# A local-attention stage in blocks of 32 queries and 64 keys: half as many probability transposes, twice as many small value products

## The chip, the cores and the metric

The kernel runs on one core of a Trainium2 chip. The metric is the device time of one execution in microseconds, the median of three runs. A profiled execution gives a span (first to last instruction) and a trace. Engines: PE is TensorE (matrix products and transposes), PEld its weight loads, DVE VectorE, ACT ScalarE, POOL GpSimd, SP the engine that issues the DMAs here.

## The reference, cut to what matters

A first attention layer, then six layers of a larger attention and a feed-forward block. The change touches the first attention alone:

```python
# x: (2, 1024, 128), 16 heads of 8, window of 32 keys
qkv = x @ W_attn + b_attn
q, k, v = jnp.split(qkv, 3, axis=-1)
scores = jnp.einsum('bhtd,bhsd->bhts', q, k) * scale
mask = causal & (j >= i - 32)
scores = jnp.where(mask[None, None], scores, -jnp.inf)
attn = jax.nn.softmax(scores, axis=-1)
out = jnp.einsum('bhts,bhsd->bhtd', attn, v)
return out.transpose(0, 2, 1, 3).reshape(b, t, c) @ W_proj + b_proj
```

A query sees itself and the 32 keys before it, so a block of 32 queries sees 64 keys, and a block of 64 queries sees 96.

## The kernel before, in words

The 2048 rows are 16 tiles of 128 (`TILES`). The first attention works through them in a software pipeline: the order on each engine is written out by hand in that engine's `tile_first`, and semaphores (names with `a_`) join the engines. Tiles 0, 1, 14 and 15 are unrolled, the rest is a loop of two tiles (`tiles`). `t` is the tile, `p` its buffer (t mod 2), `G` one of two groups of eight heads, `b` one of two groups of four inside it.

For one tile, in order of data:

- PE `project_first` (L1089, L1090) makes q, k and v from the input that ACT copied (`copy_first`, L433). ACT `qkv_first` moves them out: q (L463), k (L467), v (L471). v goes to `v_nat`, with two buffers. POOL `split_keys` (L348) makes four masked copies of the keys.
- SP `move_first` copies v from `v_nat` to `vw1`, where each query half finds its 96 keys on partitions 0 to 95: two DMAs for the tile itself (L238, L239), and one (L242) with its last 32 rows, for the next tile. L242 waits until the tile before is fully weighed (`a_pv`), since its buffer is that tile's. ACT may write v of tile t+2 into `v_nat` only when L242 of tile t has landed (`a_before`).
- PE `scores_first` adds a mask through an identity product in bf16 (L1052, 384 columns, one for each of two PSUM banks), then the scores (L1059): 2 halves of 64 queries x 2 banks, each with 4 heads x 96 keys.
- DVE `maxima_first` (L721) takes the row maxima, ACT `exps_first` (L478) one exponential per head (128x96) with its sum, 16 a tile.
- PE `transpose_probs_first` (L1067) transposes each head's 128x96 probabilities, 16 a tile, in four groups; DVE `probs_first` (L729) copies each group of four out of PSUM.
- PE `weigh_first` (L1080) multiplies by the values: a product per head and half, 96 keys deep, 64 queries x 8 columns, 32 a tile. All results of a tile stand in one PSUM bank, `OB`.
- DVE `heads_out_first` (L735, L738) divides by the sums, PE transposes (L1095), ACT moves it out (`oT`, L487), PE projects (L1099), DVE adds the bias (L745).

A product of f32 operands appears in the trace as two records, a transpose as one.

On PE one step of the pipeline is: project(t+2), transpose probabilities of (t, G=0), weigh (t-1, G=1), scores (t+1, G=0), transpose out (t-1), scores (t+1, G=1), project out (t-1), weigh (t, G=0), transpose probabilities of (t, G=1). On ACT it is: exponentials of (t, 0) second half, (t, 1), then q, k, v of t+2, the copy of the input, `oT` of t-1, and exponentials of (t+1, 0) first half.

Of the kernel before, what the change touches and what calls it, by code (L numbers as in the profile page):

```python
# [6 lines left out]
TILES = B * N // P  # L7
# [8 lines left out]
SPAN = HALF + WIN  # L16

# [17 lines left out]
def build(nc, x, Wa, ba, Wp, bp, Wqkv, Wo, scales, W1, W2, par, rope, ident, identb, mask, select, out):  # L35
# [3 lines left out]
    with ctx:  # L39
# [26 lines left out]
        msk = sb("msk", [P, TILES, SPAN], mybir.dt.uint16)  # L66

# [46 lines left out]
        pT = sb("pT", [SPAN, 8, P])  # L114
# [20 lines left out]
        PROB1, PT1 = (prob[:, :, :], prob1), (pT[:, :, :], pT1)  # L135
# [19 lines left out]
        a_seen, a_before = [sem("a_seen0"), sem("a_seen1")], [sem("a_before0"), sem("a_before1")]  # L155
        a_linv, a_o, a_ot_full, a_ot_evac = sem("a_linv"), sem("a_o"), sem("a_ot_full"), sem("a_ot_evac")
# [9 lines left out]
        pt_full, pt_evac, pv_done = sem("pt_full"), sem("pt_evac"), sem("pv_done")  # L166
        v_seen = [sem("v_seen0"), sem("v_seen1")]
# [10 lines left out]
        CONSTS = 16 * 9  # L178
# [40 lines left out]

        block = ctx.enter_context(nc.Block())  # L220
# [3 lines left out]
        def _(eng):  # L224
# [4 lines left out]
            for dst, src in ((idf[:, :], ident), (idb[:, :], identb), (wa, Wa), (wp, Wp),  # L229
                             (bias_c[:, :], ba), (bias_p, bp), (msk[:, :, :], mask),  # L230
                             (rope0[:, :, :, :], rope), (sel[:, :], select)):
# [67 lines left out]
        def _(eng):  # L299
# [8 lines left out]
            nc.gpsimd.memset(vw1[0:WIN, 0, 0, :], 0.0).then_inc(init_done, 1)  # L308
# [106 lines left out]
        def _(eng):  # L415
# [43 lines left out]
            def qkv_first(t, p):  # L459
# [9 lines left out]
                at_least(eng, a_seen[p], seen(t, p) - 32)  # L469
                at_least(eng, a_before[1 - p], t * 8 - (0 if p == 0 else 8))  # L470
# [12 lines left out]
            def heads_out_first(t):  # L483
# [3 lines left out]
                nc.scalar.activation(oT[:, 0, 0:P], RING[4][:, 0:P], ACT.Identity, bias=bias_c[:, 2:3]).then_inc(a_ot_evac, 1)  # L487
# [58 lines left out]
            exps_first(0, 0, 0, 0)  # L546

            def tile_first(t, n, p, opening, closing):

                ahead = not (isinstance(n, int) and n >= TILES - 2)  # L550
                exps_first(t, p, 0, 1)
# [9 lines left out]
                if not closing:  # L561
                    exps_first(t + 1, 1 - p, 0, 0)
            tiles(eng, tile_first, lambda t, n, p: heads_out_first(t), 0)
# [126 lines left out]
        def _(eng):  # L690
# [27 lines left out]
            def maxima_first(t, p, G):  # L718
                for b in range(2):
                    eng.wait_ge(a_s, t * 2 + (G + 1))  # L720
                    nc.vector.tensor_reduce(nmax[:, p, 8 * G + 4 * b:8 * G + 4 * b + 4],  # L721
                                            S1[G][b][:, 0:4 * SPAN].rearrange("p (h k) -> p h k", h=4),
                                            AX.X, ALU.max, negate=True).then_inc(a_max, 1)

            def probs_first(t, G, b):

                eng.wait_ge(a_pt_full, t * 4 + (2 * G + b + 1))
                at_least(eng, a_pv, t * 2 + (G - 1))
                nc.vector.tensor_copy(PT1[G][:, 4 * b:4 * b + 4, :],  # L729
                                      RING[4 + 2 * b][0:SPAN, :].rearrange("p (h q) -> p h q", h=4)).then_inc(a_pt_evac, 1)  # L730
# [12 lines left out]
            def residual_first(t, n):  # L743
                eng.wait_ge(a_wo, t + 1)
                nc.vector.tensor_tensor(y_nat[:, n, :], RING[6][:, 0:C], bias_p, ALU.add).then_inc(a_y, 1)  # L745
# [88 lines left out]
            def tile_first(t, n, p, opening, closing):  # L834
                ahead = not (isinstance(n, int) and n >= TILES - 2)
                probs_first(t, 0, 0)
# [4 lines left out]
                probs_first(t, 0, 1)  # L841
                if not closing:
                    maxima_first(t + 1, 1 - p, 0)
                if not opening:
                    residual_first(t - 1, n - 1)
                if not closing:
                    maxima_first(t + 1, 1 - p, 1)
                if not opening:
                    eng.wait_ge(a_y, t)
                    nc.vector.bn_stats(stats[:, n - 1, :], y_nat[:, n - 1, :])  # L850
                probs_first(t, 1, 0)
                probs_first(t, 1, 1)
# [177 lines left out]
        def _(eng):  # L1030
# [15 lines left out]
            def scores_first(t, n, p, G):  # L1046
# [4 lines left out]
                for b in range(2):  # L1051
                    nc.tensor.matmul(S1[G][b][:, 0:4 * SPAN], idb[:, :].bitcast(bf16),  # L1052
                                     msk[:, n, :].bitcast(bf16).rearrange("p (o k) -> p o k", o=1).to_broadcast([P, 4, SPAN]),
                                     start=True, stop=False, skip_group_check=True)
# [9 lines left out]
            def transpose_probs_first(t, G, b):  # L1064
                eng.wait_ge(a_p, t * 4 + (2 * G + b + 1))
# [397 lines left out]
```

## Time and profile before

| | us |
|---|---|
| runs: median (lowest to highest) | 2088.4 (2085.85 to 2089.87) |
| profiled execution: its own time | 2085.3 |
| its span | 2083.4 |
| first attention: first projection to last residual | 19.6 to 161.6 |
| PE busy over the whole span | 1911.9 (92%) |
| ACT, DVE, POOL busy | 1597.1, 1582.3, 1670.8 |

The first attention is 142 us of 2083.4, under 7%. The granted clock of PE is a column of its own in several views: 1.00 is 2.4 GHz, 0.50 is 1.2 GHz. "Issue" is time in which an engine waited for nothing that the profile shows. Records of matrix products are pipelined: one that is 200 ns long does not hold the engine for 200 ns, so the distance from start to start of two groups is the measure used below.

### The profile page before, as it was taken

How to read it: one execution, taken by the hardware profiler on the slowest of the kernel's cores; microseconds unless marked ns; L12 is line 12 of the kernel's file. 1: busy time of each engine (PE TensorE's matmuls, PEld its weight loads, DVE VectorE, ACT ScalarE, POOL GpSimd, SP SyncE). 2: the span in 40 equal slices, each digit the busy share in tenths (PEclk: the TensorE clock that was granted, in tenths of full speed). 3: DMA queues.
4: the chain of work that ended last, by engine and by line, in shares of the span. 5: the costliest groups of instructions: out<-in, count | busy, mean ns of one | idle time of the engine just before them, and what ended most of it. 6: DMA issues, size and time to landing. Idle time of an engine off the chain costs nothing.

```text
span 2083.4 us, 67375 instructions
## 1 busy us (share of the span) xinstructions
PE 1911.9 (92%) x22192; PEld 1446.7 (69%) x22192; DVE 1582.3 (76%) x4021; ACT 1597.1 (77%) x5607; POOL 1670.8 (80%) x1264
## 2 busy tenths in 40 slices
PE   6994999988999988999988999998999999999987
PEld 4662777874777774777774777774777774777773
DVE  5766888867888866788866788876788876888875
ACT  5872888875888874888884888884888884888873
POOL 3224999967999966999966999976899975999971
PEclk8995999999999999999999999999999999999999
DMA  3001212212112112111211211111211110211110
GB/s 118 12 12 27 69 46 49 56 32 68 49 45 58 48 32 71 48 45 45 58 34 49 69 46 45 45 47 40 75 49 45 45 47 20 65 46 45 45 44 21
DMA packets 44548, 99.44 MB, mean 48 GB/s; under 512 B 7344, under 2 KB 24208, under 8 KB 43504
## 3 DMA queue, kind: packets, MB, share of 16 engines
q1 hardware_dynamic: 44400, 97.59, 18.0%
q8 instruction: 78, 1.28, 0.2%
q14 instruction: 70, 0.57, 0.1%
HBM read 19.59 MB, written 1.05 MB: 10 GB/s over the span
## 4 chain that ended last, share of the span: by engine, by line
PE 71%; issue 11%; POOL 8%; ACT 5%; DVE 4%; DMA 0%; ACTq 0%; POOLq 0%; DVEq 0%
PE bank L1162 9%; PE bank L1175 8%; PE bank L1189 7%; PE bank L1210 7%; PE bank L1155 7%; PE bank L1191 6%; PE bank L1190 6%; PE bank L1196 6%; PE bank L1146 3%; ACT kT L533 2%; PE bank L1291 2%; POOL rn L327 2%; POOL ropeL L360 2%; POOL tsum L329 2%; PE bank L1202 2%
## 5 line engine op out<-in xcount | busy, mean ns | idle before, releaser
L327 POOL TENSOR_TENSOR rn<-n2c,half_neg 128x8 f32<-128x8 f32 x384 | 636.7, 1658 | 80.3 <-DVE n2c L807 79.6
L495 ACT ACTIVATE prob<-bank,nmax 128x96 f32<-128x96 f32 x1536 | 502.6, 352 | 131.8 <-DVE nmax L757 131.6
L329 POOL TENSOR_TENSOR tsum<-tc_,ts_ 128x512 f32<-128x512 f32 x384 | 489.6, 1275 | 0.0
L332 POOL TENSOR_TENSOR w_nat<-tsum,rn 128x512 f32<-128x512 f32 x384 | 401.3, 1045 | 37.7 <-POOL tsum L329 15.1
L800 DVE TENSOR_REDUCE n<-nat 128x8 f32<-128x512 f32 x384 | 262.3, 683 | 140.4 <-ACT nat L511 128.1
L495 ACT ACTIVATION_READ_ACCUMULATOR prob<-bank,nmax 128x1 f32 x1536 | 333.2, 217 | 0.0
L757 DVE TENSOR_REDUCE nmax<-bank 128x4 f32<-128x384 f32 x384 | 196.3, 553 | 155.4 <-PE bank L1155 147.4
L504 ACT ACTIVATE pT<-bank 96x512 f32<-96x512 f32 x384 | 230.6, 601 | 74.5 <-PE bank L1162 72.2
L1189 PE MATMUL bank<-w_hi,xs 128*128 128x512 f32 x576 | 275.7, 479 | 12.4 <-DVE ts_ L810 9.8
L1162 PE MATMUL bank<-idf,prob 128*96 128x128 f32 x1536 | 246.0, 284 | 44.1 <-ACT kT L533 28.3
L810 DVE TENSOR_TENSOR ts_<-bank,ropeL 128x256 f32<-128x256 f32 x768 | 286.1, 414 | 0.0
L803 DVE TENSOR_TENSOR tc_<-bank,ropeL 128x512 f32<-128x512 f32 x384 | 261.3, 680 | 0.0
L511 ACT ACTIVATE nat<-bank 128x512 f32<-128x512 f32 x384 | 232.9, 607 | 33.6 <-PE bank L1191 30.0
L1196 PE MATMUL bank<-idf,w_nat 128*128 128x128 f32 x1536 | 237.9, 278 | 13.1 <-POOL w_nat L332 11.6
L1196 PEld LDWEIGHTS bank<-idf,w_nat 128*128 128x128 f32 x1536 | 181.4, 141 | 90.7 <-issue 32.8
L1162 PEld LDWEIGHTS bank<-idf,prob 128*96 128x96 f32 x1536 | 159.5, 128 | 106.6 <-ACT kT L533 79.2
L1190 PE MATMUL bank<-w_lo,xs 128*128 128x512 f32 x576 | 229.2, 398 | 0.0
L1191 PE MATMUL bank<-w_hi,xs_lo 128*128 128x512 f32 x576 | 229.2, 398 | 0.0
L1175 PE MATMUL bank<-vspace,pT 96*64 96x64 f32 x6144 | 221.2, 225 | 0.0
L1175 PEld LDWEIGHTS bank<-vspace,pT 96*64 96x64 f32 x6144 | 194.7, 138 | 31.4 <-issue 20.7
L1210 PE MATMUL bank<-oT,wo 128*128 128x128 f32 x1536 | 207.3, 279 | 4.1 <-ACT oT L524 4.1
L1210 PEld LDWEIGHTS bank<-oT,wo 128*128 128x128 f32 x1536 | 189.5, 194 | 6.0 <-ACT oT L524 5.5
(124 smaller groups left out, 3349.2 us busy)
## 6 DMA issues: line engine op xcount, KB each, us to landing
vspace<-v_nat SPq DMA_DIRECT2D x96, 384.0 KB, 4.0
vspace<-v_nat SPq DMA_DIRECT2D x96, 256.0 KB, 3.4
vspace<-v_nat SPq DMA_DIRECT2D x95, 128.0 KB, 2.2
nat<-w_qkv SPq DMA_DIRECT2D x5, 1536.0 KB, 8.4
wo<-w_o SPq DMA_DIRECT2D x6, 512.0 KB, 3.9
w<-w SPq DMA_DIRECT2D x6, 341.0 KB, 3.1
shared<-w_qkv SPq DMA_DIRECT2D x1, 1536.0 KB, 8.6
w<-w SPq DMA_DIRECT2D x6, 192.0 KB, 3.0
```

The lines of the kernel that those rows point to most:

```text
L327: nc.gpsimd.tensor_tensor(rn[:, r, :], n2c[:, r, :], half_neg[:, 0:8], ALU.pow).then_inc(pool_step, 1)
L329: nc.gpsimd.tensor_tensor(tsum[:, r, :], tc_[:, r, :], ts_[:, r, :], ALU.add).then_inc(pool_step, 1)
L332: nc.gpsimd.tensor_tensor(w_nat[:, r, :].rearrange("p (h d) -> p h d", d=D), tsum[:, r, :].rearrange("p (h d) -> p h d", d=D), rn[:, r, :] ...
L495: last = nc.scalar.activation(prob[:, 4 * b + i, :], SB[b][:, i * SPAN:(i + 1) * SPAN], ACT.Exp, bias=nmax[:, p, 8 * G + 4 * b + i:8 * G + ...
L810: last = nc.vector.tensor_tensor(ts_[:, r, :].rearrange(heads3, d=D)[:, :, lo:lo + D // 2], pj[:, :].rearrange(heads3, d=D)[:, :, hi:hi + ...
L1162: last = nc.tensor.transpose(RING[at][0:SPAN, i * P:(i + 1) * P], prob[:, 4 * b + i, :], idf[:, :])
L1175: last = nc.tensor.matmul(OB[qs, a:a + D], pT[:, 4 * b + i, qs], vw[:, p, half, head * D:(head + 1) * D], start=True, stop=True, skip_grou ...
L1189: nc.tensor.matmul(PJ[x % 2][:, :], xs[:, p, :], hi, start=True, stop=False)
L1190: nc.tensor.matmul(PJ[x % 2][:, :], xs[:, p, :], rest, start=False, stop=False)
L1191: nc.tensor.matmul(PJ[x % 2][:, :], xs_lo[:, p, :], hi, start=False, stop=True).then_inc(pj_ready, 1)
L1196: last = nc.tensor.transpose(RING[at][:, i * P:(i + 1) * P], w_nat[:, j % 2, i * P:(i + 1) * P], idf[:, :])
L1210: last = nc.tensor.matmul(YB[:, 0:P], wo[:, 4 * G + i, :], oT[:, G, i * P:(i + 1) * P], start=G == 0 and i == 0, stop=G == 1 and i == 3)
```

## The change

The first attention goes to blocks of 32 queries and 64 keys (`BLOCKS` = 4, `SEEN` = 64).

- Mask and scores have 4 x 64 = 256 columns instead of 384; the score products of a group are 8 instead of 4 (four blocks x two banks), 32 queries each. A second mask table `mskB` is loaded at the start, one more DMA.
- Exponentials and maxima work on 64 keys per head. ACT puts the probabilities of head i of b=0 and head i of b=1 side by side, so that one 128x128 transpose takes two heads: 8 transposes a tile instead of 16, 2 DVE copies instead of 4. Partitions 0 to 63 hold the heads of b=0, 64 to 127 those of b=1.
- Value products are one per head and block, 64 keys deep, 32 queries x 8 columns: 64 a tile instead of 32. The two partition halves write the same bank, so they go in two turns (b=0, then b=1), and the second waits for the end of the first (`a_pv_half`). A semaphore `pv_begun` is incremented ahead of each turn, and nobody waits for it.
- `move_first` fills the blocks of values with 8 DMAs instead of 2, and the rows for the next tile with 2 instead of 1.
- The order on PE, ACT and DVE is written anew: the transposes of (t, 0) wait for all eight exponentials of their group, and the two turns of (t-1, 1) stand on either side of scores (t+1, 0). On ACT both halves of the exponentials of (t+1, 0) now end the step. `oT` and the projected output change places in the PSUM banks 4 and 6.

```diff
-        vw1 = first_only(4 * C)[0:SPAN, :].rearrange("p (r h c) -> p r h c", r=2, h=2)
-        prob1 = first_only(8 * SPAN).rearrange("p (h k) -> p h k", h=8)
-        pT1 = first_only(8 * P)[0:SPAN, :].rearrange("p (h q) -> p h q", h=8)
+        vw1 = first_only(4 * C).rearrange("p (r w c) -> p r w c", r=2, w=BLOCKS)
+        prob1 = first_only(8 * SEEN)
+        pT1 = first_only(4 * P).rearrange("p (h q) -> p h q", h=4)
...
                 eng.wait_ge(a_v, t + 1)
                 at_least(eng, a_pv, t * 2 - 2)
-                eng.dma_start(vw1[WIN:SPAN, p, 0, :], v_nat[0:HALF, p, 0:C]).then_inc(a_seen[p], 16)
-                eng.dma_start(vw1[:, p, 1, :], v_nat[WIN:P, p, 0:C]).then_inc(a_seen[p], 16)
+                for b in range(2):
+                    cols = slice(b * C // 2, (b + 1) * C // 2)
+                    eng.dma_start(vw1[b * SEEN + WIN:(b + 1) * SEEN, p, 0, :], v_nat[0:WIN, p, cols]).then_inc(a_seen[p], 16)
+                    for w in range(1, BLOCKS):
+                        eng.dma_start(vw1[b * SEEN:(b + 1) * SEEN, p, w, :], v_nat[(w - 1) * WIN:(w + 1) * WIN, p, cols]
+                                      ).then_inc(a_seen[p], 16)
                 if not last:
                     at_least(eng, a_pv, t * 2)
-                    eng.dma_start(vw1[0:WIN, 1 - p, 0, :], v_nat[P - WIN:P, p, 0:C]).then_inc(a_before[1 - p], 16)
+                    for b in range(2):
+                        eng.dma_start(vw1[b * SEEN:b * SEEN + WIN, 1 - p, 0, :],
+                                      v_nat[P - WIN:P, p, b * C // 2:(b + 1) * C // 2]).then_inc(a_before[1 - p], 16)
...
-                at_least(eng, a_pt_full, t * 4 + (2 * G + b - 3))
+                at_least(eng, a_pt_full, t * 2 + (G - 1))
                 for i in range(4):
-                    head = 8 * G + 4 * b + i
+                    head, slot = 8 * G + 4 * b + i, 2 * i + b
                     last = nc.scalar.activation(
-                        PROB1[G][:, 4 * b + i, :], S1[G][b][:, i * SPAN:(i + 1) * SPAN], ACT.Exp,
+                        PROB1[G][:, slot * SEEN:(slot + 1) * SEEN], S1[G][b][:, i * SEEN:(i + 1) * SEEN], ACT.Exp,
...
-                for half in range(2):
-                    qs, ks = slice(half * HALF, (half + 1) * HALF), slice(half * HALF, half * HALF + SPAN)
+                for w in range(BLOCKS):
+                    qs, ks = slice(w * WIN, (w + 1) * WIN), slice(w * WIN, w * WIN + SEEN)
                     for b in range(2):
                         rows = slice((2 * G + b) * ROWS, (2 * G + b + 1) * ROWS)
-                        last = nc.tensor.matmul(S1[G][b][qs, 0:4 * SPAN].rearrange("p (h k) -> p h k", h=4),
+                        last = nc.tensor.matmul(S1[G][b][qs, 0:4 * SEEN].rearrange("p (h k) -> p h k", h=4),
...
-            def transpose_probs_first(t, G, b):
-                eng.wait_ge(a_p, t * 4 + (2 * G + b + 1))
+            def transpose_probs_first(t, G):
+
+                eng.wait_ge(a_p, t * 4 + (2 * G + 2))
                 for i in range(4):
-                    last = nc.tensor.transpose(RING[4 + 2 * b][0:SPAN, i * P:(i + 1) * P], PROB1[G][:, 4 * b + i, :], idf[:, :])
+                    last = nc.tensor.transpose(RING[4 + 2 * G][:, i * P:(i + 1) * P],
+                                               PROB1[G][:, 2 * i * SEEN:2 * (i + 1) * SEEN], idf[:, :])
...
+            def weigh_first(t, p, G, b):
+
+                if b == 0:
+                    at_least(eng, a_pv, t * 2 + G)
+                    eng.wait_ge(a_pt_evac, t * 2 + (G + 1))
+                    if G == 0:
+                        at_least(eng, a_o, t)
+                        eng.wait_ge(a_seen[p], seen_block(t, p))
+                        at_least(eng, a_before[p], prev_block(t, p))
+                else:
+                    eng.wait_ge(a_pv_half, t * 2 + (G + 1))
+
+                eng.sem_inc(pv_begun, 1)
+                rows = slice(b * SEEN, (b + 1) * SEEN)
+                for i in range(4):
+                    head = 8 * G + 4 * b + i
+                    for w in range(BLOCKS):
+                        qs = slice(w * WIN, (w + 1) * WIN)
+                        last = nc.tensor.matmul(OB[qs, head * DA:(head + 1) * DA], PT1[G][rows, i, qs],
+                                                vw1[rows, p, w, (4 * G + i) * DA:(4 * G + i + 1) * DA], start=True, stop=True,
...
```

On PE, the rest of the step of tile 1 after its projections, before. `vspace` and `prob` hold probabilities, `msk` the mask, `shared` the keys:

```order
L1067 MATMUL bank<-idf,prob 96x128 x8
L1080 MATMUL bank<-vspace 64x8 x16
L1052 MATMUL bank<-msk,idb 128x384 x2
L1059 MATMUL bank<-shared,qT 64x384 x4
L1095 MATMUL bank<-idf,o_nat 128x128
L1052 MATMUL bank<-msk,idb 128x384 x2
L1059 MATMUL bank<-shared,qT 64x384 x4
L1099 MATMUL bank<-vspace,oT 128x128
L1080 MATMUL bank<-vspace,pT 64x8 x16
L1067 MATMUL bank<-idf,vspace 96x128 x8
```

The same step of the changed program:

```order
L1085 MATMUL bank<-idf,prob 128x128 x4
L1107 MATMUL bank<-vspace 32x8 x16
L1069 MATMUL bank<-mskB,idb 128x256 x2
L1076 MATMUL bank<-shared,qT 32x256 x8
L1107 MATMUL bank<-vspace 32x8 x16
L1069 MATMUL bank<-mskB,idb 128x256 x2
L1076 MATMUL bank<-shared,qT 32x256 x8
L1122 MATMUL bank<-idf,o_nat 128x128
L1107 MATMUL bank<-vspace,pT 32x8 x16
L1126 MATMUL bank<-vspace,oT 128x128
L1107 MATMUL bank<-vspace,pT 32x8 x16
L1085 MATMUL bank<-idf,vspace 128x128 x4
```

Two groups of products became four turns, and both groups of scores stand ahead of the transpose of the output. On SP, the DMAs of values of tiles 0 and 1, before:

```order
L238 DMA vspace<-v_nat 64x128
L239 DMA vspace<-v_nat 96x128
L242 DMA vspace<-v_nat 32x128
L238 DMA vspace<-v_nat 64x128
L239 DMA vspace<-v_nat 96x128
L242 DMA vspace<-v_nat 32x128
```

The same two tiles of the changed program:

```order
L253 DMA vspace<-v_nat 32x64
L255 DMA vspace<-v_nat 64x64 x3
L253 DMA vspace<-v_nat 32x64
L255 DMA vspace<-v_nat 64x64 x3
L260 DMA vspace<-v_nat 32x64 x2
L253 DMA vspace<-v_nat 32x64
L255 DMA vspace<-v_nat 64x64 x3
L253 DMA vspace<-v_nat 32x64
L255 DMA vspace<-v_nat 64x64 x3
L260 DMA vspace<-v_nat 32x64 x2
```

Three DMAs a tile became ten, and the release of a `v_nat` buffer (L242, now L260) is two DMAs long.

## Rows read from the trace of the kernel before

**Rows 1.** The page: busy time, share of the span, instructions of each engine.
```profile
PE 1911.9 (92%) x22192; PEld 1446.7 (69%) x22192; DVE 1582.3 (76%) x4021; ACT 1597.1 (77%) x5607; POOL 1670.8 (80%) x1264
```

**Rows 2.** Busy time by stretches: from:to, length, engines (records), granted clock, DMA.
```profile
124.90:132.80 7.90, 7.85 (x111) 5.47 (x110) 5.72 (x13) 6.45 (x40) 1.25 (x1) 1.00 0.05 12
```

**Rows 3.** Timeline of one step: start, length, engine, line, idle before.
```profile
96.86 0.28 ACT L471 ACTIVATE v_nat<-bank 128x128 f32<-128x128 f32 x1 [1.45 <-DMA vspace<-v_nat]
...
97.48 0.34 ACT L478 ACTIVATE prob<-bank,nmax 128x96 f32<-128x96 f32 x1
...
97.74 0.46 PE L1099 MATMUL bank<-vspace,oT 128*128 128x128 f32 x2
...
98.13 1.10 PE L1080 MATMUL bank<-vspace,pT 96*64 96x8 f32 x32
...
99.92 0.26 ACT L478 ACTIVATION_READ_ACCUMULATOR prob<-bank,nmax 128x1 f32 x1
...
100.08 0.61 PE L1089 MATMUL bank<-vspace 128*128 128x128 f32 x4
...
100.75 1.15 PE L1067 MATMUL bank<-idf,prob 128*96 128x128 f32 x8
...
101.25 0.39 PEld L1067 LDWEIGHTS bank<-idf,prob 128*96 128x96 f32 x4 [0.15 <-issue]
...
101.82 1.10 PE L1080 MATMUL bank<-vspace 96*64 96x8 f32 x32
...
102.86 0.50 PE L1052 MATMUL bank<-msk,idb 128*128 x2
102.97 0.53 SPq L242 DMA_DIRECT2D vspace<-v_nat  x1
...
103.29 0.88 PE L1059 MATMUL bank<-shared,qT 32*64 32x384 f32 x8
...
104.09 0.33 PE L1095 MATMUL bank<-idf,o_nat 128*128 128x128 f32 x1
...
104.76 0.28 ACT L471 ACTIVATE v_nat<-bank 128x128 f32<-128x128 f32 x1 [1.49 <-DMA vspace<-v_nat]
```

**Rows 4.** L471 (v out of PSUM): what it waits for; then L242: its landing.
```profile
  DMA vspace<-v_nat: 18.9, 13
...
DMA to landing us min/median/max: 1.7/1.8/1.8
```

**Rows 5.** The page: a group of ACT copies, 128x512.
```profile
L511 ACT ACTIVATE nat<-bank 128x512 f32<-128x512 f32 x384 | 232.9, 607 | 33.6 <-PE bank L1191 30.0
```

**Rows 6.** Records of L1059 alone, in a short stretch: length, PE busy (records), clock, DMA.
```profile
95.42:95.45 0.03, 0.03 (x4) 1.00 0.00 0
```

**Rows 7.** Timeline of PE at a granted clock of 0.50.
```profile
25.92 0.82 PE L1052 MATMUL bank<-msk,idb 128*128 128x384 bf16 x2
...
28.16 1.22 PE L1089 MATMUL bank<-vspace 128*128 128x128 f32 x4
...
29.60 1.92 PE L1067 MATMUL bank<-idf,prob 128*96 128x128 f32 x8
31.30 0.85 PE L1052 MATMUL bank<-msk,idb 128*128 128x384 bf16 x2
...
152.29 1.88 PE L1080 MATMUL bank<-vspace,pT 96*64 96x8 f32 x32
...
154.11 1.94 PE L1067 MATMUL bank<-idf,vspace 128*96 128x128 f32 x8
```

**Rows 8.** Busy time by stretches, at the end of the stage.
```profile
149.00:151.00 2.00, 1.23 (x33) 1.03 (x33) 1.01 (x4) 0.71 (x5) 0.00 (x0) 1.00 0.03 8
151.00:153.00 2.00, 1.45 (x17) 1.20 (x17) 0.77 (x3) 0.37 (x1) 0.00 (x0) 0.65 0.00 0
```

**Rows 9.** Timeline: the two PE instructions ahead of the fall of the clock.
```profile
150.75 0.30 PE L1095 MATMUL bank<-idf,o_nat 128*128 128x128 f32 x1 [0.77 <-DVE o_nat L738]
...
151.60 0.76 PE L1099 MATMUL bank<-vspace,oT 128*128 128x128 f32 x2 [0.55 <-ACT oT L487]
```

More of the change, by code:

```diff
@@ L32, with build @@
 COLUMN = [0, INNER, HB, 2 * INNER, INNER + HB, 2 * INNER + HB]
-def build(nc, x, Wa, ba, Wp, bp, Wqkv, Wo, scales, W1, W2, par, rope, ident, identb, mask, select, out):
+def build(nc, x, Wa, ba, Wp, bp, Wqkv, Wo, scales, W1, W2, par, rope, ident, identb, mask, mask_block, select, out):
     f32, f32r, bf16 = mybir.dt.float32, mybir.dt.float32r, mybir.dt.bfloat16
@@ L218, in prev_in, with seen_block, prev_block @@
             return t * 8 + (0 if p == 0 else 8)
+        def seen_block(t, p):
+            return 4 * seen(t, p)
+        def prev_block(t, p):
+            return 2 * prev_in(t, p)
         block = ctx.enter_context(nc.Block())
@@ L468, in qkv_first @@
                                      ).then_inc(a_k, 1)
-                at_least(eng, a_seen[p], seen(t, p) - 32)
-                at_least(eng, a_before[1 - p], t * 8 - (0 if p == 0 else 8))
+                at_least(eng, a_seen[p], seen_block(t, p) - 128)
+                at_least(eng, a_before[1 - p], t * 16 - (0 if p == 0 else 16))
                 nc.scalar.activation(v_nat[:, p, 0:C], QKV[:, 2 * P:3 * P], ACT.Copy).then_inc(a_v, 1)
@@ L486, in heads_out_first @@
                 at_least(eng, a_wo, t)
-                nc.scalar.activation(oT[:, 0, 0:P], RING[4][:, 0:P], ACT.Identity, bias=bias_c[:, 2:3]).then_inc(a_ot_evac, 1)
+                nc.scalar.activation(oT[:, 0, 0:P], RING[6][:, 0:P], ACT.Identity, bias=bias_c[:, 2:3]).then_inc(a_ot_evac, 1)
             def exps(t, p, G, b):
@@ L744, in residual_first @@
                 eng.wait_ge(a_wo, t + 1)
-                nc.vector.tensor_tensor(y_nat[:, n, :], RING[6][:, 0:C], bias_p, ALU.add).then_inc(a_y, 1)
+                nc.vector.tensor_tensor(y_nat[:, n, :], RING[4][:, 0:C], bias_p, ALU.add).then_inc(a_y, 1)
             def copy_prev_first(t, n, p):
@@ L835, in tile_first @@
                 ahead = not (isinstance(n, int) and n >= TILES - 2)
-                probs_first(t, 0, 0)
+                probs_first(t, 0)
+                if not closing:
+                    maxima_first(t + 1, 1 - p, 0)
                 if not opening:
@@ L840, in tile_first @@
                     copy_prev_first(t + 2, n + 2, p)
[L841 to L845, printed above, removed]
                 if not closing:
@@ L1068, in transpose_probs_first @@
                 last.then_inc(a_pt_full, 1)
-            def weigh_first(t, p, G):
-                eng.wait_ge(a_pt_evac, t * 4 + (2 * G + 2))
-                if G == 0:
-                    at_least(eng, a_o, t)
-                    eng.wait_ge(a_seen[p], seen(t, p))
-                    at_least(eng, a_before[p], prev_in(t, p))
-                for h in range(8):
-                    head = 8 * G + h
-                    for half in range(2):
-                        qs = slice(half * HALF, (half + 1) * HALF)
-                        last = nc.tensor.matmul(OB[qs, head * DA:(head + 1) * DA], PT1[G][:, h, qs],
-                                                vw1[:, p, half, head * DA:(head + 1) * DA], start=True, stop=True,
+            def weigh_first(t, p, G, b):
[16 more added lines that the diff above has]
+                                                vw1[rows, p, w, (4 * G + i) * DA:(4 * G + i + 1) * DA], start=True, stop=True,
@@ L1082, in weigh_first @@
                                                 skip_group_check=True)
-                last.then_inc(a_pv, 1)
+                last.then_inc(a_pv if b else a_pv_half, 1)
             def project_first(t, p):
@@ L1094, in transpose_out_first @@
                 eng.wait_ge(a_o, t + 1)
-                nc.tensor.transpose(RING[4][:, 0:P], o_nat[:, 0, 0:C], idf[:, :]).then_inc(a_ot_full, 1)
+                nc.tensor.transpose(RING[6][:, 0:P], o_nat[:, 0, 0:C], idf[:, :]).then_inc(a_ot_full, 1)
             def project_out_first(t):
                 eng.wait_ge(a_ot_evac, t + 1)
-                nc.tensor.matmul(RING[6][:, 0:C], oT[:, 0, 0:P], wp, start=True, stop=True).then_inc(a_wo, 1)
+                nc.tensor.matmul(RING[4][:, 0:C], oT[:, 0, 0:P], wp, start=True, stop=True).then_inc(a_wo, 1)
             def tile_first(t, n, p, opening, closing):
@@ L1420, in _constants @@
     mask = np.where(seen[None] & ((key >= 0)[None] | (tile > 0)), 0.0, -1e30).transpose(1, 0, 2).astype(f)
+    row, kk = i % WIN, np.arange(SEEN)[None, :]
+    block = (kk >= row) & (kk <= row + WIN)
+    there = (kk >= WIN) | (i >= WIN)
+    mask_block = np.where(block[None] & (there[None] | (tile > 0)), 0.0, -1e30).transpose(1, 0, 2).astype(f)
     eye = np.eye(P, dtype=f)
@@ L1434 @@
     A = np.ascontiguousarray
-    rope, eye, eyeb, mask = _constants()
+    rope, eye, eyeb, mask, mask_block = _constants()
     def swap(s):
@@ L1449 @@
     w2[:, :FF] = np.asarray(L0_ffn_W2)
+    wa = np.array(L0_attn_W_attn)
+    wa[:, 2 * C:] = wa[:, 2 * C:].reshape(C, 2, 2, 4, DA).transpose(0, 2, 1, 3, 4).reshape(C, C)
     ins = {
-        "x": A(np.asarray(L0_attn_x).reshape(B * N, C)), "w_attn": A(L0_attn_W_attn),
+        "x": A(np.asarray(L0_attn_x).reshape(B * N, C)), "w_attn": A(wa),
         "b_attn": A(np.asarray(L0_attn_b_attn).reshape(3, C).T), "w_proj": A(L0_attn_W_proj),
@@ L1454 @@
         "w_o": A(L0_ffn_Wo), "scales": scales, "w_1": A(L0_ffn_W1), "w_2": w2, "vectors": par, "rope": rope,
-        "identity": eye, "identity_bf16": eyeb, "mask": mask, "select": np.tile(np.repeat(np.eye(PER_ROW, dtype=np.float32), DA, 0), (P // ROWS, 1)),
+        "identity": eye, "identity_bf16": eyeb, "mask": mask, "mask_block": mask_block, "select": np.tile(np.repeat(np.eye(PER_ROW, dtype=np.float32), DA, 0), (P // ROWS, 1)),
     }
```

75 lines of the change are left out of this document (38 added, 37 removed).

## The prediction, made before the changed kernel ran

> **What bounds the kernel now.** I read the page first: PE is busy for 92% of the span [rows 1]. Then the chain of waits for the first 165 us, which from 43 us on is nearly all PE. Then the stretches: in 7.90 us PE is busy for 7.85, at a granted clock of 1.00, so 2.4 GHz; ACT for 6.45, DVE for 5.72 [rows 2]. Last the timeline of one step of the stage, 96.86 to 104.76, so 7.90 us from one L471 to the next [rows 3]. PE has work without a pause.
>
> But a second thing closes at the same time. ACT stands still for 1.45 us in each step before it may write v (L471): it waits for the DMA that frees `v_nat`, 13 times, 18.9 us in total [rows 3, 4]. So thirteen steps form a loop: L471, `oT`, project out, weigh (t,0), transpose (t,1), projections, transpose (t+1,0), weigh (t,1), DMA L242, L471. All of it but the DMA and ACT's part is PE's work. A smaller PE share shortens it only until another branch closes it: the exponentials.
>
> **The change, part by part, at full clock.**
>
> Exponentials. 512 columns take 607 ns on ACT, 128 take 280 [rows 3, 5], so 0.85 ns a column; 32 columns fewer save 0.027 us. Before, eight of them begin at 97.48 and end at 99.92 + 0.26 = 100.18, 3.32 us after L471 starts. After: 3.32 - 8 x 0.027 = 3.10. The transposes of (t+1,0) now need all eight, where before the first group needed four.
>
> Transposes. A group of four and the switch to the next kind takes 101.82 - 101.25 = 0.57 us [rows 3]. There are two groups a tile instead of four: about 1.0 us less PE work.
>
> Scores. From L1052 to L1059 it is 0.43 us, from there to L1095 0.80: 1.23 for a group [rows 3]. Four records of L1059 start within 0.03 us [rows 6], so the four pieces of the array (two row halves of this group, two column halves) work side by side, and the 0.80 is two rounds of 384 columns and an end. With 256 columns a mask saves 0.05 and a round 0.11: 0.43 - 0.11 + 0.80 - 0.21 = 0.91, if eight pieces work side by side as four do. If only four do, there are four rounds of 0.27 instead of two, 1.45, and the loop is 8.4.
>
> Value products. 32 records take 102.86 - 101.82 = 1.04 us: sixteen steps of 0.058 and 0.11 at the end, if a pair of column halves goes side by side. A turn of the new order has 32 records too, in eight steps of four pieces. With weights of 32 columns instead of 64 a step is near 0.032: a turn 0.37 us. By the number of records it would be 1.04, since 32 records take that now; no steps saved at all gives 0.58. I take 0.37, the row's own mechanism, and keep 1.04 as the upper end.
>
> By the Trainium skill (TensorE: Matmul & The Clock Gate, "Back-to-back issue gap") a product below some 64 columns costs a floor of about 25 ns from start to start, however small. The 32 records in 1.04 us are 32 ns each and don't contradict it, while the four within 0.03 us do [rows 3, 6]. By it a turn would be about 0.9 us; this is rival C.
>
> DMAs. L242 takes SP 0.53 us and lands 1.8 us after its start [rows 3, 4]. Now two of them stand there: the second starts 0.53 later, so v is free 2.33 us after the end of the weighing instead of 1.8. The eight of the next tile follow on SP behind these: 5.3 us for all ten, in a step of 7.8, and their values are needed by the weighing more than a step later. They hide; without that cover a step could not be shorter than 5.3 + 1.8 = 7.1, which the loop exceeds anyway.
>
> DVE loses 2 copies of 0.69 and some maxima and isn't the bound. The extra constant adds one issue of some 0.5 us and 256 KB ahead of PE's first instruction. PE then runs ahead of ACT, which waits for memsets of POOL until 16 us; I cost it at 0, at most 0.9.
>
> The loop, from one L471 to the next: 3.10 (exponentials) + 0.06 + 0.57 (transposes) + 0.37 (first turn) + 0.91 (scores, which now stand between the turns, where before nothing stood) + 0.37 + 0.11 (second turn and its end) + 2.33 (DMAs) = 7.82 us. Against 7.90 that is no gain worth naming. PE's own work falls to 0.67 (projections) + 1.1 + 4 x 0.37 + 1.82 + about 0.55 (transpose out, project out) = 5.6 us of 7.82; it is idle for 2.2: about 1.5 waiting for `oT`, whose ACT instruction stands behind L471, and the rest for the exponentials. So the work saved on PE turns into idle time.
>
> **The clock.** What idle time does here is seen at the end of the stage. PE is busy for 1.23 of the 2.00 us from 149, with small value products, one transpose and pauses of 0.77 and 0.55 us, and the clock goes from 1.00 to 0.50 at about 151.6 [rows 8, 9]. In the whole steady part it stays at 1.00 [rows 2]. The changed step has a longer pause (1.5 us) in each of the thirteen steps, with a transpose, a turn, a pause, a small projection and another turn around it, so a stretch like 149 to 151 or emptier recurs every step. I expect the clock to fall within the first steps at full clock, and to come back only now and then: at the start PE works without a pause from 25.92 to 31.30 and is still at 1.2 GHz [rows 7].
>
> The Trainium skill (TensorE: Matmul & The Clock Gate, "Why this matters for your kernels") names long idle gaps alone as what lowers the clock, and by that rule this stage would stay at 2.4 GHz: rival B. The trace doesn't agree, as it fell behind pauses of 0.77 and 0.55 us [rows 9].
>
> The step at 1.2 GHz. Projections 29.60 - 28.16 = 1.44. Transposes of four: (31.30 - 29.60) / 2 + 0.1 = 0.95. Scores: 28.16 - 25.92 = 2.24, less twice the savings of full clock, 2 x (0.11 + 0.21): 1.60. Value products: 154.11 - 152.29 = 1.82 for 32 records, sixteen steps of 0.107 and 0.1; eight of 0.054 and the end 0.55 to 0.6: 0.6. Project out 152.29 - 151.60 = 0.69 [rows 3, 7, 9]. Now PE's branch closes the loop: `oT` is done 0.88 us behind L471 (97.74 - 96.86), then 0.69 + 0.6 + 0.95 + 1.44 = 4.56 at the transposes, which is later than the 3.16 of the exponentials; then 0.95 + 0.6 + 1.60 + 0.6 + 0.15 + 2.33 = 10.8 us a step.
>
> With seven of ten steps at 1.2 GHz the mean is 0.7 x 10.8 + 0.3 x 7.82 = 9.9 us, 2.0 more than 7.9; thirteen steps: +26 us. The share of seven in ten is a choice: a fall within one or two steps at full clock, and four or so until it comes back. The last two tiles have no L471 to wait for and less PE work, -1. Sum +25. The profiled execution's own time is 2085.3 (its span 2083.4, and 1.9 around it), the median of the runs 2088.4; I add to the middle of the two, 2086.9, here and below: 2112.
>
> **Rivals.**
>
> A (forecast): the clock is low for most of the stage, 2112. If it never comes back, 13 x 2.9 - 1 = +37: 2124. If it is low for a third of the steps, 13 x 0.9 - 1 = +11: 2098.
>
> B: the clock holds and the loop through the DMAs is all there is: 13 x (7.82 - 7.90) - 2 for the closing tiles, which are then faster too = -3: 2084. For it: the clock doesn't fall before 151 in this trace. Against it: the step's pauses, as above.
>
> C: small products are bound by their number. A turn is 1.04 us, and two lie in the loop: 7.82 + 1.34 = 9.16 us a step. PE's work is then 5.6 + 2.7 = 8.3 of 9.16 and the clock holds: 13 x 1.26 = +16, so 2103. Against it: [rows 6].
>
> D, the other side: the loop through v isn't closed as I reckon, because ACT reaches L471 late enough that the DMAs have landed. Then ACT's work decides: 6.45 - 16 x 0.027 = 6.0 us a step [rows 2], 13 x -1.9 = -25: 2062. It decides from the point where the weighing of (t-1,1) ends more than 2.33 us ahead of L471. For it: PE's work of 5.6 us would allow it. Against it: the weighing stands behind the transposes, which stand behind all exponentials of their group, and those behind L471.
>
> That the change doesn't do what it says has no chance worth a number: the halved transposes stand in the program's order.
>
> **Numbers.** A 0.55, C 0.15, B 0.16, D 0.14. A change of under 0.2% (4.2 us) can't be told from none here. A and C are slower: 0.70. B is mostly within 0.2%: 0.15, and 0.01 faster. D is faster: 0.14. So faster 0.15, same 0.15, slower 0.70. The range takes in B, C and nearly all of A, and leaves out D: 2083 to 2128, a little above the case in which the clock never comes back, as the runs of before differ by 4. A's own range, for eight in ten of its cases, is 2097 to 2126.
>
> **What would show it.** Right: idle time of PE ahead of project out of about 1.5 us where the clock is 1.00; a granted clock of 0.50 in many of the steps between 35 and 150 us; ACT's wait before v at 1.8 us or more; the second L260 of a pair landing near 2.3 us after the end of the weighing; 0.9 us for a group of scores at full clock. A turn of 32 records well above 0.4 us at full clock points to C. Steps near 7.8 us and a clock of 1.00 throughout: B. Steps near 6 us with no wait before v: D, and the forecast is wrong. It is also wrong if the time is lost outside the first 170 us.

## The result: 1.4% slower, and the profile after

| | before | after |
|---|---|---|
| runs: median (lowest to highest), us | 2087.1 (2078.8 to 2089.9) | 2115.1 (2112.6 to 2117.2) |
| ratio, 95% interval | | 1.0137 (1.0110 to 1.0164) |
| profiled execution: own time, span | 2085.3, 2083.4 | 2115.8, 2114.0 |
| v written for tiles 2 and 15 | 32.2, 136.3 | 30.3, 164.4 |
| first product of the next layers | 185.8 | 212.5 |

The column before has one run more than the three of the opening section. Medians here and below are of the fast runs: one of the four runs of experiment 2 took 2208.2 us at a mean granted clock of 0.835, where its others had 0.944 to 0.961, and is left out.

The forecast was 2112 us. PE's busy time has risen by 11 us on the page, although it got fewer columns to work on [rows 1]:

```profile
PE 1923.0 (91%) x23344; PEld 1451.9 (69%) x23344; DVE 1557.3 (74%) x3989; ACT 1591.4 (75%) x5607; POOL 1671.2 (79%) x1264
```

Thirteen steps from tile 2 to tile 15 took 104.1 us before (8.00 each) and 134.1 after (10.32 each), +30. The opening gives 2.0 back and the close 1.4, which makes the +26.7 at the next layers; the last 4 us of the span lie in code that didn't change and are less than the runs of one kernel differ by. So the loss lies in the stage that was changed.

The stretches of after (from:to, length, busy time and records of PE, PEld, DVE, ACT, POOL, granted clock, DMA). Before, the same stage has 1.00 in the clock's column [rows 2]:

```profile
35.00:160.00 125.00, 106.12 (x2204) 73.53 (x2206) 49.23 (x133) 75.47 (x456) 28.89 (x18) 0.61 0.06 13
93.00:109.00 16.00, 14.59 (x261) 10.69 (x261) 5.74 (x15) 11.45 (x72) 3.57 (x2) 0.50 0.07 15
```

The clock is at 1.2 GHz for most of the stage. One step of it in the timeline, which answers to [rows 3] and [rows 7] (start, length, engine, line, idle before):

```profile
92.72 0.28 ACT L490 ACTIVATE v_nat<-bank 128x128 f32<-128x128 f32 x1 [3.82 <-DMA vspace<-v_nat]
93.60 0.77 PE L1126 MATMUL bank<-vspace,oT 128*128 128x128 f32 x2 [1.22 <-ACT oT L506]
94.29 0.61 PE L1107 MATMUL bank<-vspace,pT 64*32 64x8 f32 x32
94.84 1.11 PE L1085 MATMUL bank<-idf,vspace 128*128 128x128 f32 x4
95.74 1.06 PE L1116 MATMUL bank<-vspace 128*128 128x128 f32 x4
97.02 1.06 PE L1085 MATMUL bank<-idf,prob 128*128 128x128 f32 x4
98.01 0.61 PE L1107 MATMUL bank<-vspace 64*32 64x8 f32 x32
98.56 0.61 PE L1069 MATMUL bank<-mskB,idb 128*128 x2
99.10 1.10 PE L1076 MATMUL bank<-shared,qT 32*32 32x256 f32 x16
100.13 0.61 PE L1107 MATMUL bank<-vspace 64*32 64x8 f32 x32
100.68 0.61 PE L1069 MATMUL bank<-mskB,idb 128*128 x2
100.81 1.18 SPq L260 DMA_DIRECT2D vspace<-v_nat  x2
103.21 0.28 ACT L490 ACTIVATE v_nat<-bank 128x128 f32<-128x128 f32 x1 [4.17 <-DMA vspace<-v_nat]
```

From one L490 to the next it is 10.49 us. Read it as a ring: v written, `oT`, project out, a turn, transposes, projections, transposes, turn, scores, turn, the two L260, v again. PE waits only at L1126, and ACT for four microseconds on the DMA, where it waited 1.5 [rows 3]. Over the stage that wait has grown from 18.9 us [rows 4] to (view of L490, idle time by what ended it):

```profile
  DMA vspace<-v_nat: 50.9, 13
```

This step is at 1.2 GHz from its pause on, and so are the first of the thirteen and two more. In the other nine the clock comes back for about a third of the step, ahead of the pause in front of L1126, and is lost again in that pause. In the step before the one above:

```profile
89.50:92.50 3.00, 2.39 (x99) 1.15 (x83) 2.09 (x7) 0.00 (x0) 0.92 (x1) 1.00 0.03 6
```

There the new pieces can be measured at 2.4 GHz:

```profile
89.78 0.44 PE L1107 MATMUL bank<-vspace 64*32 64x8 f32 x32
90.15 0.39 PE L1069 MATMUL bank<-mskB,idb 128*128 x2
90.47 0.66 PE L1076 MATMUL bank<-shared,qT 32*32 32x256 f32 x16
91.28 0.33 PE L1122 MATMUL bank<-idf,o_nat 128*128 128x128 f32 x1
```

A turn takes 90.15 - 89.78 = 0.37 us, mask to scores 0.32.

### The profile page after: what moved, and what is told of

Same layout as the page of the kernel before. It is cut to its first block, busy times and chain, and to the rows that moved or that the text cites. A ratio compares the mean times of both kernels' runs of the same rounds, so it can differ in the third digit from the quotient of the medians.

```text
span 2114.0 us, 69731 instructions
## 1 busy us (share of the span) xinstructions
PE 1923.0 (91%) x23344; PEld 1451.9 (69%) x23344; DVE 1557.3 (74%) x3989; ACT 1591.4 (75%) x5607; POOL 1671.2 (79%) x1264
## 4 chain that ended last, share of the span: by engine, by line
PE 70%; issue 11%; POOL 7%; ACT 5%; DVE 3%; DMA 2%; SPq 1%; ACTq 0%; POOLq 0%; DVEq 0%
PE bank L1184 9%; PE bank L1197 8%; PE bank L1211 7%; PE bank L1232 7%; PE bank L1177 7%; PE bank L1213 6%; PE bank L1212 6%; PE bank L1218 6%; PE bank L1168 3%; ACT kT L552 2%; PE bank L1313 2%; POOL rn L346 2%; POOL ropeL L379 2%; POOL tsum L348 2%; PE bank L1224 2%
```

## The experiments

The theory on trial (called K in the expectations, A in the prediction): the longer release of `v_nat` makes a pause on PE, the clock falls, and the half clock makes the loss. Rivals: the wait itself costs the time; the small products do; the order of the turns does. Every ratio is against the kernel before, run on the same chip beside it, whose medians were 2085.0 to 2089.2.

**1. The changed kernel with PE kept at work.** Eight bf16 products of 384 columns, whose results nobody reads, stand ahead of project out:

```diff
+                    for _ in range(8):
+                        nc.tensor.matmul(OB[:, C:4 * C], idb[:, :].bitcast(bf16), msk[:, 0:4, :].bitcast(bf16), start=True,
+                                         stop=True, skip_group_check=True)
```

> The changed kernel with eight extra bf16 products (384 columns each, 0.163 us each at 2.4 GHz) in PE's pause ahead of project out; nobody reads their results. Theory K (the loss is the half clock that the pauses bring): the clock stays at or near 1.00 between 35 and 150 us, a step takes 7.8 to 8.2 us instead of 10.3, and the time falls to 2082 to 2092 although work was added. Rival R (the loss is the two-DMA release of the value buffer and the longer waits, the low clock only accompanies them): no gain, or 8 x 0.16 to 0.33 us a step dearer, 2115 to 2135.

Measured 2091.7 us, 1.0029 (1.0013 to 1.0044). With work added, the kernel is 23 us faster than after. Seven steps in the middle, at a granted clock of 1.00:

```profile
86.00:142.00 56.00, 52.09 (x1329) 32.92 (x1331) 28.68 (x78) 41.93 (x259) 15.64 (x11) 1.00 0.08 16
```

56 us for seven steps is 8.0 each, where after needs 10.3. With the clock held in most of the stage at most 6 of the 28 us are left, though there is more work; the other 22 go with the clock.

**2. The turns back to back** (the changed kernel, the second turn of (t-1, 1) ahead of the scores):

```diff
+                    weigh_first(t - 1, 1 - p, 1, 1)
                     scores_first(t + 1, 0)
-                if not opening:
-                    weigh_first(t - 1, 1 - p, 1, 1)
```

> The changed kernel with the two turns of value products of (t-1,1) back to back, and scores (t+1,0) behind them instead of between them. By my loop the scores lay in it: it is shorter by 0.9 us at full clock, 1.6 at half, less about 0.2 for the second turn's wait. At half clock PE's own work of about 10 us closes it first: a step of 9.8 to 10.0 instead of 10.3, 2108 to 2111; if the denser PE brings the clock back more often, down to 2095. Rival R: the release starts 0.9 to 1.6 us earlier and all of it is gained, 2096 to 2103. If the order between the turns was hiding a wait that I don't see, it is slower than 2115.

Measured 2108.8, 1.0107 (1.0067 to 1.0148), as expected. The order is worth some 6 us, not the loss, and even these aren't clear of noise, since the intervals of the two ratios overlap. One step at full clock is 7.32 us (136.88 - 129.56, from one v to the next), yet most of the stage is at half clock, here for 54 us on end while PE is busy for all but 1.3:

```profile
71.00:125.00 54.00, 52.68 (x981) 35.26 (x981) 22.61 (x60) 34.65 (x209) 14.46 (x9) 0.50 0.07 14
```

**3. The kernel before with a release of two DMAs, and nothing else:**

```diff
-                    eng.dma_start(vw1[0:WIN, 1 - p, 0, :], v_nat[P - WIN:P, p, 0:C]).then_inc(a_before[1 - p], 16)
+                    for c in (slice(0, C // 2), slice(C // 2, C)):
+                        eng.dma_start(vw1[0:WIN, 1 - p, 0, c], v_nat[P - WIN:P, p, c]).then_inc(a_before[1 - p], 16)
```

> The kernel before, with the DMA that frees the value buffer (L242) split in two of half the columns, as the change has it; nothing else changed. Theory K: the release is 0.53 us later, ACT's wait goes from 1.45 to about 2.0, PE gets a pause of about 0.6 us a step but stays busy for 7.8 of 8.4 us, the clock holds, time 2087 + 13 x 0.5 = 2094. Rival R (the DMAs carry the loss): 2105 or more. If a pause of 0.6 us is enough to lower the clock: over 2110 with a clock of 0.50 in the stage.

Measured 2115.2, 1.0135 (1.0096 to 1.0175): the whole loss, without the new blocks, the halved transposes or the turns. I had expected the clock to hold, and 2094. Two steps that follow each other, then the pause of PE (a step holds one) and ACT's next two writes of v:

```profile
93.90:102.40 8.50, 7.78 (x113) 5.43 (x109) 5.72 (x13) 6.40 (x37) 1.47 (x2) 1.00 0.05 12
102.40:114.00 11.60, 10.87 (x113) 8.31 (x109) 5.82 (x13) 6.53 (x37) 3.35 (x2) 0.71 0.03 8
```

```profile
93.88 0.28 ACT L472 ACTIVATE v_nat<-bank 128x128 f32<-128x128 f32 x1 [3.61 <-DMA vspace<-v_nat]
94.76 0.46 PE L1100 MATMUL bank<-vspace,oT 128*128 128x128 f32 x2 [0.72 <-ACT oT L488]
102.42 0.28 ACT L472 ACTIVATE v_nat<-bank 128x128 f32<-128x128 f32 x1 [2.12 <-DMA vspace<-v_nat]
114.00 0.28 ACT L472 ACTIVATE v_nat<-bank 128x128 f32<-128x128 f32 x1 [4.40 <-DMA vspace<-v_nat]
```

The same 113 records of PE take 8.5 us in one step and 11.6 in the next. Both steps have the pause (0.72 us, then 0.73 ahead of 103.30); behind the first the clock holds, behind the second it falls, and comes back some seven microseconds later. The stretches behind the second pause:

```profile
102.40:104.00 1.60, 0.87 (x16) 0.61 (x14) 0.09 (x1) 1.57 (x10) 1.60 (x1) 1.00 0.20 51
104.00:106.00 2.00, 2.00 (x32) 1.95 (x30) 1.33 (x4) 1.74 (x12) 0.49 (x1) 0.51 0.00 0
...
110.00:112.00 2.00, 2.00 (x39) 1.54 (x42) 0.54 (x3) 0.00 (x0) 0.00 (x0) 0.79 0.00 0
```

The second DMA costs 8.54 - 7.90 = 0.64 us a step directly (102.42 - 93.88 = 8.54), some 8 us in thirteen steps. The rest of the 28 us, about two and a half times as much, comes through the clock.

The Trainium skill (TensorE: Matmul & The Clock Gate, "Why this matters for your kernels") asks for TensorE to be kept busy and warns of long idle gaps between bursts. By it a pause of 0.72 us would do no harm. The trace disagrees: in this step it is enough. The same page's section "A second HAM failure mode: psum-queue depth-cycling" tells of a kernel whose clock went up and down with short idle times between groups of products, and with that this trace agrees.

**4. The same with four filler products** ahead of project out, as in 1:

> The kernel before with the split release DMA (as e7_before_release2, which was 30 us slower) and four extra bf16 products of 384 columns in PE's pause of 0.72 us ahead of project out. Theory K: the pause was all that lowered the clock; filled, the clock stays at 1.00 up to the end of the stage, each step is 8.4 to 8.6 us, time 2091 to 2096. Rival R (the DMA itself disturbs the step): nothing changes or the work comes on top, 2112 to 2125.

Measured 2093.6, 1.0034 (1.0023 to 1.0046): 21.5 us back by adding work. The products fill the pause whole:

```profile
94.71 0.82 PE L1121 MATMUL bank<-msk,idb 128*128 128x384 bf16 x4
95.51 0.46 PE L1100 MATMUL bank<-vspace,oT 128*128 128x128 f32 x2
```

```profile
60.00:140.00 80.00, 80.00 (x1067) 53.71 (x1060) 53.15 (x122) 60.45 (x349) 23.09 (x15) 1.00 0.05 12
```

Thus 7 to 9 of the old kernel's lost 28 us belong to the loop (1.0034 is 7 us, the two medians differ by 8.7) and the rest to the clock. The second DMA is still there, so it isn't the DMA itself that lowers the clock.

**5. Unrolled, nothing else** (after; a control for 6 to 12, which need an unrolled loop to address four buffers):

```diff
-                    with eng.Fori(1, TILES // 2 - 1) as i:
...
+                    for n in range(TILES):
+                        move_first(n, n % 2, n == TILES - 1)
```

> Control for e3_v4: the changed kernel with its first attention unrolled over all 16 tiles and still two buffers for v. If unrolling has no part in the gain of e3_v4, this runs like the changed kernel: steps of 10 to 10.5 us, 2112 to 2117. If it has, it is well below 2110.

Measured 2112.4, 1.0120 (1.0096 to 1.0144): unrolling changes nothing that can be told.

**6. Four buffers for v**, so that ACT doesn't wait for the release (after, unrolled):

```diff
-                at_least(eng, a_seen[p], seen_block(t, p) - 128)
-                at_least(eng, a_before[1 - p], t * 16 - (0 if p == 0 else 16))
-                nc.scalar.activation(v_nat[:, p, 0:C], QKV[:, 2 * P:3 * P], ACT.Copy).then_inc(a_v, 1)
+                at_least(eng, a_seen[p], seen_block(t, p) - 256)
+                at_least(eng, a_before[1 - p], t * 16 - (32 if p == 0 else 48))
+                o = t // 2 % 2 * C
+                nc.scalar.activation(v_nat[:, p, o:o + C], QKV[:, 2 * P:3 * P], ACT.Copy).then_inc(a_v, 1)
```

> The changed kernel with its first attention unrolled and four buffers for v instead of two, so that ACT may write v two tiles before the DMA that frees the old buffer. Theory K with the loop through L471/L490: ACT's wait before v is gone, PE is no longer idle behind it, the clock holds, a step takes 6.2 to 6.6 us (exponentials, transposes, a turn, scores, a turn, DVE, transpose out, oT), the time is 2062 to 2070. Rival R: the wait is gone as well and the step is near 6.4, the same time, so these two differ in e1 only. Rival N (small products and transposes alone let the clock fall, however dense): clock 0.50, PE's own work of about 10 us is the step, 2108 to 2113.

Measured 2082.2, 0.9976 (0.9960 to 0.9991). The loss is gone (5 has 2112.4), so ACT's wait for the release carries it in the changed kernel too; but the 15 us more that were expected aren't there. Steps are 6.4 to 7.2 us at full clock and about 9 at half, 7.86 in the mean. The granted clock is 0.79 in the mean:

```profile
35.00:133.00 98.00, 88.08 (x2210) 61.87 (x2210) 48.81 (x133) 75.81 (x462) 28.89 (x18) 0.79 0.09 19
```

**7. Four buffers for v in the kernel before** (unrolled, the same edit there):

```diff
-                at_least(eng, a_before[1 - p], t * 8 - (0 if p == 0 else 8))
+                at_least(eng, a_before[1 - p], t * 8 - (16 if p == 0 else 24))
```

> The kernel before, unrolled and with four buffers for v. ACT's wait of 1.45 us before v goes. PE's own work of 7.8 us a step is the bound, so a step is 7.75 to 7.85 instead of 7.88, the clock stays full, and the time is 2083 to 2086. If the loop through the DMA and not PE's work had bound the kernel before, steps of 7.3 or less, under 2080.

Measured 2082.1, 0.9972 (0.9956 to 0.9988), with 7.70 us a step. PE has no idle time left:

```profile
60.00:123.00 63.00, 63.00 (x905) 44.56 (x903) 45.83 (x106) 54.43 (x307) 19.29 (x12) 1.00 0.06 15
```

So with v free the old blocks are bound by PE, and the new ones (6) are no faster. Something else holds them.

**8. Four buffers for v and four filler products** (6 plus 1, with `range(4)`):

> Four buffers for v (as e3_v4) and four extra bf16 products of 384 columns (0.65 us a step at 2.4 GHz) in PE's pause ahead of project out; nobody reads them. e3_v4 had steps of 6.4 to 7.2 us where the clock was full and about 9 where it was half. Theory K: with the pause filled the clock is full far more often than in e3_v4, a step averages 6.8 to 7.2 us against 7.86, time 2067 to 2076. Rival (the DMAs of values, ten a step, are now the bound and not the clock): the clock rises but the steps stay near 7.8, or the added work costs 0.3 to 0.6 us a step, 2082 to 2090.

Measured 2087.8, 1.0005 (0.9992 to 1.0019); the expected gain didn't come, and it is 6 us slower than 6. The clock was higher (0.88 in the stage), and the steps still 8.0 us. The rival of the expectation was right; the view of the value products (L1109), idle time by what ended it:

```profile
  issue: 27.4, 53
  DMA vspace<-v_nat: 11.8, 8
```

PE waited eight times for the value DMAs (in 6 it was six times, 7.8 us), which may start only when the buffer they fill has been weighed.

**9. Four buffers for the arranged values `vw1` too** (6 and):

```diff
-        vw1 = first_only(4 * C).rearrange("p (r w c) -> p r w c", r=2, w=BLOCKS)
+        vw1 = first_only(8 * C).rearrange("p (r w c) -> p r w c", r=4, w=BLOCKS)
...
-                at_least(eng, a_pv, t * 2 - 2)
+                at_least(eng, a_pv, t * 2 - 6)
...
-                    at_least(eng, a_pv, t * 2)
+                    at_least(eng, a_pv, t * 2 - 4)
```

> Four buffers for v and four for the blocks of values (vw1), so that none of the ten DMAs a step waits for the weighing of the tile before; order, products and exponentials as in the changed kernel. Reading of e8_v4_filler: its steps were held by value DMAs that can only start after the weighing, up to 2.1 us of PE waiting for them. If so: no PE wait for DMA, steps of 6.3 to 6.8 us at full clock, a mean of 6.8 to 7.4 with some time at half clock, time 2066 to 2078. Rival (SP's ten issues, 5.3 us and more a step, are the bound however early they may start): steps of 7 to 8, 2080 to 2088.

Measured 2074.3, 0.9939 (0.9921 to 0.9958), as expected: faster than both kernels, 7.40 us a step in the mean. The value products wait for a DMA once, for 1.1 us. The clock is still low in places:

```profile
35.00:127.00 92.00, 86.37 (x2226) 59.60 (x2226) 49.04 (x133) 75.41 (x464) 28.91 (x18) 0.83 0.10 21
```

**10. The same with four filler products:**

> As e10_v4w4, with four extra bf16 products (0.65 us at 2.4 GHz) ahead of project out. If the clock is still low at times in e10_v4w4, this keeps it at 1.00: steps of 6.6 to 6.9, 2065 to 2072. If the clock holds by itself there, the products cost 0 to 0.3 us a step and this is 0 to 4 us slower than e10_v4w4.

Measured 2075.0, 0.9937 (0.9916 to 0.9958), 7.44 us a step: no gain, where 2065 to 2072 were expected if the clock is low in 9. The clock is higher, 0.94 where 9 has 0.83, but the value products wait for their DMAs again (view of L1110, in 9 and then here):

```profile
  DMA vspace<-v_nat: 1.1, 1
...
  DMA vspace<-v_nat: 6.8, 5
```

What the added work and these waits cost is about what the clock gives back. Why the DMAs come late again wasn't looked into.

**11. Number 9 with the turns back to back** (the edit of 2):

> As e10_v4w4, with the two turns of (t-1,1) back to back ahead of scores (t+1,0). The chain exponentials, transposes, turns, DVE, transpose out, oT, exponentials is then shorter by up to 0.9 us, and ACT's own 6.0 us a step closes it: steps of 6.0 to 6.4 at full clock, 2058 to 2068. Rival: the second turn's wait for the first, and oT coming later than ACT would take it, leave it as e10_v4w4 within 3 us.

Measured 2089.6, 1.0015 (0.9999 to 1.0032), 15 us more than 9, against the expectation. Two stretches of it:

```profile
50.00:80.00 30.00, 29.45 (x559) 19.09 (x543) 12.41 (x35) 18.24 (x111) 6.07 (x4) 0.50 0.08 18
86.00:104.00 18.00, 15.41 (x455) 9.60 (x455) 10.04 (x30) 13.35 (x82) 5.27 (x4) 1.00 0.08 17
```

In the first PE is busy for 98% of the time and the clock stays low, from 37 to 85 us; in the second PE is busy for 86% and the clock is full. Busy time alone doesn't decide. Part of the difference is in the measure: the same work fills more of the time at 1.2 GHz.

**12. Number 11 with four filler products:**

> e12_v4w4_turns with four extra bf16 products (384 columns) ahead of project out. e12 stood at half clock for 48 us on end with steps of 9.93 us, PE's own work at 1.2 GHz, though PE was hardly ever idle there; at full clock its steps were 7.3 to 7.9. If the extra products, which stream without a break, bring the clock back and hold it: steps of 6.3 to 7.4, 2062 to 2076. If what is missing at half clock isn't work in the pauses, the products add 1.3 us to each step of 9.93 and it is 2095 to 2108.

Measured 2077.9, 0.9944 (0.9921 to 0.9966), 12 us faster than 11 by added work (15 by the two ratios), and 2 us above the expected range:

```profile
35.00:130.00 95.00, 86.72 (x2234) 58.55 (x2236) 47.95 (x133) 74.12 (x454) 28.96 (x18) 0.96 0.10 21
```

The column is 1.00 too early in this view: the trace has no record of the clock ahead of 46.6 us, and the products themselves are at 1.2 GHz until then (1.46 us for four that take 0.82 at 2.4 GHz in 4):

```profile
42.68 1.46 PE L1149 MATMUL bank<-msk,idb 128*128 128x384 bf16 x4
```

From 46.6 us on the clock is full but for two short stretches, near 82 and near 113 us. PE is busy for less of its time than in 11's slow stretch. So more columns streamed in each step brought the clock back, where PE had hardly any idle time to fill. The Trainium skill (TensorE: Matmul & The Clock Gate, "Part 4: PE-mode transpose") says that transposes don't count as busy PE for the clock in the way that other products do. The runs don't show that this is the reason here: in the old step transposes and small value products take (100.08 - 98.13) + (102.86 - 100.75) = 4.06 of 7.90 us [rows 3], and its clock stays at 1.00.

## Why the prediction was right

**The loop.** The ring and its order were as predicted, and its wait is where it was predicted: on ACT ahead of v. The two L260 free v 103.21 - 100.81 = 2.40 us after the first starts; predicted 2.33.

**The pieces at full clock.** A turn 0.37, as predicted, so rival C (1.04) is out. By the Trainium skill (TensorE: Matmul & The Clock Gate, "Back-to-back issue gap") a small product costs 25 ns at the least, which for 32 records makes 0.8, an estimate. The records stand 0.37 / 32 = 12 ns apart in the mean, in groups of four that start within 0.03 us, so the trace disagrees where four pieces of the array work side by side. Records of the value products, then of the scores, alone in a short stretch:

```profile
89.78:89.81 0.03, 0.03 (x4) 0.03 (x5) 1.00 0.00 0
...
90.47:90.52 0.05, 0.05 (x8) 0.05 (x12) 1.00 0.00 0
```

Scores were predicted at 0.91 a group if eight pieces go together, and at 1.45 if only four do; eight start within 0.05 us. The timeline of experiment 9 has a whole group at full clock, from its mask to the next turn, 65.15 - 64.23 = 0.92:

```profile
64.23 0.39 PE L1072 MATMUL bank<-mskB,idb 128*128 128x256 bf16 x2
64.56 0.66 PE L1079 MATMUL bank<-shared,qT 32*32 32x256 f32 x16
65.15 0.44 PE L1110 MATMUL bank<-vspace 64*32 64x8 f32 x32
```

**The clock.** The step on which the forecast hung: the clock falls in the first steps and is low for most of the stage. It did (0.61 in the mean), so rival B is out. The loss by the clock is shown by 1 and 4. It came back more often than I thought, in nine of thirteen steps, but never for a whole one. The pause was predicted at 1.5 us behind work at full clock; in those nine steps it was 2.0 and 1.6 in the first two and 1.20 to 1.27 in the other seven. In three of the steps at half clock throughout it was 0.81 to 0.84, in the first step 1.8.

**The step at half clock.** Predicted 10.8, measured 10.49. To the transposes 97.02 - 92.72 = 4.30 instead of 4.56, since the projections took 1.28, the transposes 0.90 and a turn 0.55 instead of 1.44, 0.95 and 0.6; then 0.99, 0.55, 1.57 and 0.55 instead of 0.95, 0.6, 1.60 and 0.6; then 2.53 instead of 2.48.

**The share.** Seven steps in ten at half clock were a choice and not worked out from rows, and they gave a mean of 9.9. It was 10.32, and the full-clock steps of 7.82 never came: the first two steps took 11.3 and 11.4 us, and the other eleven 9.7 to 10.5, most of them partly at full clock. The thirteen steps cost 30, not 26. The opening gave 2.0 back, which I had at nothing, and the close 1.4 for my 1. These misses largely cancel, which is luck: +26.7 at the next layers for a forecast of +25.

**Where the reasoning was too narrow.** I named the clock's fall as the work of thinner PE work and a pause of 1.5 us together, and charged the second DMA only with 0.53 us in the loop. Experiment 3 shows that the DMA is enough by itself: the old kernel stood at the edge, and a pause of 0.72 us in an otherwise full step took it over. That a change of the old kernel would have lost the same 28 us was in none of the cases.

**Rival D** was right in one thing: PE's work would allow a step well under 7.8 us. Two more buffers each for v and for `vw1` open that way (9), and then steps of 6.4 to 7.4 at full clock appear. It was wrong that the changed kernel would go there by itself.

**Open.** What exactly makes the clock fall and return isn't settled; the runs show single cases on either side, and the filler products both fill a pause and add columns. Whether 9 could be held at full clock without added work, and what four `vw1` buffers would do in the kernel before, wasn't tried. Nor was a release by one DMA in the new layout, where the two halves of the heads stand on different partitions.

## What to carry to other kernels

Work taken from an engine turns into idle time unless the ring that closes the step, buffers and their DMAs included, gets shorter too; so look first at which DMA frees which buffer, and free it before the work is cut. On PE such idle time may cost twice, since it can lower the clock for all that stands in the step. Test this with a few products that nobody reads: where adding work makes the kernel faster, as it did three times here (1, 4, 12), the clock is what was lost. Where it doesn't, as twice (8, 10), look at what else the step waits for.

## What the runs showed of the hardware

- A pause of 0.72 us in a step of 8.5, PE busy for 7.78 of it, was followed by a fall of the clock from 1.00 to 0.50 within 0.7 us of its end in one step and not in the step before (3); with the pause filled it stayed at 1.00 from 50 to 168 us (4).
- PE can stay at 1.2 GHz while it is busy: 52.7 of 54 us (2), 29.5 of 30 (11), in a step of transposes, small value products, masks, scores and projections. Four bf16 products of 384 columns in each step were enough to bring it back (12).
- Eight records of scores start within 0.05 us and four of value products within 0.03, so that many pieces of the array work side by side: 12 ns in the mean from one value record to the next, where the old 64-wide ones stood 1.04 / 32 = 32 ns apart [rows 3].
- A second DMA of 32 rows behind the first delays the release by 0.6 us (2.40 against 1.8 [rows 4]), about the time that SP takes more to issue the two (1.18 against 0.53 us [rows 3]).
